# Cross-attention kernel: transposes of the probabilities one by one between a key tile's context products instead of four in a row

## The chip, the cores and the metric

One core of a Trainium2 chip runs the whole program in one launch. The metric is the device time of one execution in microseconds (us), the median over several runs. Engines are called by the profile's names: PE (matrix products and transposes), PEld (the loading of PE's stationary operand, which the profile shows as an engine of its own), DVE, ACT, POOL, and SP, which issues the transfers.

## The reference, cut to what matters

Two layers, each an attention over a context of 1500 rows and a mixture of experts, work on 8 x 56 tokens of 256 channels. The change touches the softmax attention of the first layer only:

```
q = rms_norm((layernorm(x) @ Wq)  per head, 16 heads of 128)
k = rms_norm((ctx @ Wk)           per key head, 4 heads of 128)
v = ctx @ Wv                      4 heads of 128
probs = softmax(q k^T / sqrt(128))            over 1500 context rows
out   = (probs v, heads side by side) @ Wo
x     = x + out
```

All sums are in float32, and every product of full accuracy is made of three passes over operands that are split in a high and a low part.

## The kernel before, in words

The program has three stages: the sums of the second layer's linear attention and all queries; the softmax attention, one batch row after the other (`softmax_attention`); and a tail with the mixtures of experts. The second stage holds the change.

A batch row is worked off in two **units**, u = 0 and u = 1, of eight heads each; there are 16 units. Below, "even" units are those with u = 0 and "odd" ones those with u = 1. Instead of projecting values and then summing, the kernel sums the context rows themselves with the probabilities as weights (the **context products**), and projects the sums afterwards (`output`). A unit runs so:

- `scores` writes 12 tiles of scores (PE) into three banks of PSUM (`ring`). DVE (L1052) moves them to `pr` with the running minimum, ACT (L944) takes the exponentials.
- Then come 12 steps, one for each key tile t of 125 context rows. `turn(t)` transposes the probabilities of tile t with four PE transposes (L877) into bank t % 3 of `ring`. ACT (L960) copies the bank into the high part `pT[0]`, DVE (L1067) subtracts to get the low part `pT[1]`, and with that frees the bank and raises `ring_free`. The context products of step t are two times the three passes of `mm3` (L102 to L104), 448 columns each, into `csum`; PE waits for `ring_free` of tile t before them.
- The transposes run two tiles ahead: step t issues `turn(t + 2)` and then the products of t. `turn(0)` and `turn(1)` stand ahead of the steps, and steps 10 and 11 have none. So 10 groups of four transposes in a unit stand inside a step.
- At the end of most steps stands a piece of the key projection of the next unit, `key_step`, by the list `SEQ`: either six products into `proj` (then ACT L933, DVE L1018 and POOL L1118 square it and split the square), or two products into `mean` (L835), after which ACT takes logarithm and exponential (L938, L940) and DVE (L1021, L1026) and POOL (L1122) make the normalised keys. In odd units DVE also splits the next batch row's context (L998) and queries (L1006, L1009) between these. The last unit has no `key_step`.

Every engine works its list in the written order and is held by semaphores alone. In each step PE's list reads, before the change:

```
if t + 2 < KT:
    turn(t + 2)
wait(pe, ring_free, (2 * b + u) * NR + NSC + t + 1)
...
for i in range(DC):
    last = mm3(nc, csum[:, i, 0:QU], ...)
last.then_inc(pv_done, 1)
if keys and t + 2 < len(SEQ):
    key_step(*keys, *SEQ[t + 2])
```

Of the kernel before, what the change touches and what calls it, by code (L numbers as in the profile page):

```python
# [19 lines left out]
TP = NTOK // TT  # L20
# [3 lines left out]
KT = 12  # L24
KP = SK // KT
# [9 lines left out]
QU = 2 * QG  # L35
# [25 lines left out]
def wait(eng, sem, value):  # L61

    if isinstance(value, int) and value <= 0:
        return
    eng.wait_ge(sem, value)
# [34 lines left out]
def mm3(nc, out, w_hi, w_lo, x_hi, x_lo, start, stop):  # L100

    nc.tensor.matmul(out, w_lo, x_hi, start=start, stop=False, skip_group_check=True)  # L102
    nc.tensor.matmul(out, w_hi, x_lo, start=False, stop=False, skip_group_check=True)  # L103
    return nc.tensor.matmul(out, w_hi, x_hi, start=False, stop=stop, skip_group_check=True)  # L104
# [631 lines left out]
def softmax_attention(nc, qT, rz, ctx_dram, ctxT_dram, wk, wv, raw_t, ct, kk, q, ident):  # L736
# [8 lines left out]
    with ExitStack() as ctx:  # L745
        p = Phase(nc, ctx, "att")
        raw_n = p.sb("raw_n", [KP, 2, KT // 2, D])
        cn = [p.sb(f"cn{i}", [KP, KT, D], F32R) for i in range(2)]
# [3 lines left out]
        pr = p.sb("pr", [TP, 4, SK])  # L752
# [4 lines left out]
        pT = [p.sb(f"pT{i}", [KP, 3, QU], F32R) for i in range(2)]  # L757
# [4 lines left out]
        ring = p.ps("ring", [128, 3, 512])  # L762
        csum = p.ps("csum", [128, 2, 512])
# [8 lines left out]
        ring_full, ring_free = p.sem("ring_full"), p.sem("ring_free")  # L772
# [17 lines left out]
        @block.sync  # L790
        def _(sp):
            def load_t(b):
                wait(sp, t_lo, (b - 1) * PIECES)
                for c in range(KC):
                    y = slice(c * CH, (c + 1) * CH)
                    src = ctxT_dram[bass.ds(b, 1), :, y] if not isinstance(b, int) else ctxT_dram[b:b + 1, :, y]
                    sp.dma_start(raw_t[:, c], src.rearrange("a (k p) n -> p (a k) n", p=128)).then_inc(t_loaded[c], 16)

            def load_n(b):
                for half in range(2):  # L800
                    wait(sp, n_lo, (b - 1) * KT + (half + 1) * (KT // 2))
                    rows = slice(half * (SK // 2), (half + 1) * (SK // 2))
                    src = ctx_dram[bass.ds(b, 1), rows, :] if not isinstance(b, int) else ctx_dram[b:b + 1, rows, :]
                    sp.dma_start(raw_n[:, half], src.rearrange("a (j p) c -> p (a j) c", p=KP))\
                        .then_inc(n_loaded[half], 16)

            load_n(0)
            load_t(1)
            load_n(1)
            with sp.Fori(2, B) as b:  # L810
                load_t(b)
                load_n(b)

        @block.tensor
        def _(pe):
            def key_step(b, u, part, i):


                n = (2 * b + u - 1) * NS + i
                c, g = i // 2, 2 * u + i % 2  # L820
                if part == 0:
                    if u == 0 and i % 2 == 0:
                        wait(pe, t_lo, (b - 1) * PIECES + DC * (c + 1))
                    wait(pe, k_full, n - 1)
                    for d in range(DC):
                        last = mm3(nc, proj[:, i % 2, 0:CH], wk[0][:, d, g * HD:(g + 1) * HD],
                                   wk[1][:, d, g * HD:(g + 1) * HD], ct[0][:, c, d, :], ct[1][:, c, d, :], d == 0, d == DC - 1)
                    last.then_inc(proj_done, 1)
                else:
                    wait(pe, sq_lo, n + 1)  # L830
                    wait(pe, ln_done, n)
                    if i == 0:
                        wait(pe, out_free, 2 * b + u - 1)
                    for half in (1, 0):
                        last = nc.tensor.matmul(mean[:, 0:CH], mean_mat[:], sq[half][:, i % 2, :],  # L835
                                                start=(half == 1), stop=(half == 0))
                    last.then_inc(mean_done, 1)

            def output(b, u, ahead=NS):


                wait(pe, cs_lo, (2 * b + u + 1) * DC)
                wait(pe, ln_done, (2 * b + u) * NS + ahead)
                wait(pe, out_free, 2 * b + u)
                for gi in range(2):
                    w = slice((2 * u + gi) * HD, (2 * u + gi + 1) * HD)
                    x = slice(gi * QG, (gi + 1) * QG)
                    for i in range(DC):
                        last = mm3(nc, mean[:, x], wv[0][:, i, w], wv[1][:, i, w],
                                   cs[0][:, i, x], cs[1][:, i, x], i == 0, i == DC - 1)  # L850
                last.then_inc(out_full, 1)

            def scores(b, u):

                for j in range(4):
                    gi = j // 2
                    for c in range(KC):
                        r = (2 * b + u) * NR + j * KC + c
                        if j % 2 == 0:
                            wait(pe, k_lo, (2 * b + u - 1) * NS + 2 * c + gi + 1)  # L860
                        if u == 0 and j == 0 and c == 0:
                            wait(pe, q_lo, 2 * b)
                        wait(pe, ring_free, r - 2)
                        h = 8 * u + 2 * j
                        mm3(nc, ring[0:TP, c, 0:CH], q[0][:, h:h + 2, :], q[1][:, h:h + 2, :],
                            kk[:, c, gi, :], kk[:, c, 2 + gi, :],
                            True, True).then_inc(ring_full, 1)

            def unit(b, u, keys, before):


                def turn(t):
                    if t % TPC == 0:
                        wait(pe, exp_done, (2 * b + u) * NE + 3 + t // TPC + 1)
                    wait(pe, ring_free, (2 * b + u) * NR + NSC + t - 2)
                    for j in range(4):
                        last = nc.tensor.transpose(ring[0:KP, t % 3, j * TP:(j + 1) * TP],  # L877
                                                   pr[:, j, t * KP:(t + 1) * KP], ident[0:TP, 0:TP])
                    last.then_inc(ring_full, 1)

                if keys:
                    key_step(*keys, *SEQ[0])
                    key_step(*keys, *SEQ[1])
                turn(0)
                turn(1)
                if before:
                    output(*before)
                for t in range(KT):  # L890
                    if t + 2 < KT:
                        turn(t + 2)
                    wait(pe, ring_free, (2 * b + u) * NR + NSC + t + 1)
                    if u == 0:
                        wait(pe, n_lo, b * KT + t + 1)
                    if t == 0:
                        wait(pe, cs_lo, (2 * b + u) * DC)
                    for i in range(DC):
                        last = mm3(nc, csum[:, i, 0:QU], cn[0][:, t, i * 128:(i + 1) * 128],
                                   cn[1][:, t, i * 128:(i + 1) * 128], pT[0][:, t % 3, :], pT[1][:, t % 3, :],  # L900
                                   t == 0, t == KT - 1)
                    last.then_inc(pv_done, 1)
                    if keys and t + 2 < len(SEQ):
                        key_step(*keys, *SEQ[t + 2])

            def batch(b, first, last):
                scores(b, 0)
                unit(b, 0, (b, 1), None if first else (b - 1, 1))
                scores(b, 1)
                unit(b, 1, None if last else (b + 1, 0), (b, 0))  # L910

            pe.wait_ge(eps_set, 4)
            batch(0, True, False)
            with pe.Fori(1, B - 1) as b:
                batch(b, False, False)
            batch(B - 1, False, True)
            output(B - 1, 1, 0)
# [1285 lines left out]
```

## Time and profile before

| what | value |
|---|---|
| median of 3 runs | 1297.81 us (1297.76 to 1299.46) |
| the profiled execution's own time | 1295.38 us |
| its span, first to last instruction | 1293.7 us |
| mean granted TensorE clock | 0.967 |
| PE busy / PEld busy | 1185.8 us (92%) / 1042.6 us (81%) |
| DVE / ACT / POOL busy | 885.6 (68%) / 731.8 (57%) / 537.9 us (42%) |
| transposes L877 | 768, of 112x112 |
| context products L102 to L104 | 1152, of 125x448 |

Matrix instructions are pipelined: a new one starts before the one ahead of it has ended, so the distance from start to start tells what an instruction costs, and the duration doesn't. The softmax attention lies between about 372 and 1042 us of the span.

### The profile page before, as it was taken

The page shows a single profiled execution, that of the slowest core. Times are in us where ns is not written, and L with a number is a line of the kernel's source. Part 1 is how long each engine was busy: PE and PEld are TensorE (multiplying, and loading weights), DVE is VectorE, ACT ScalarE, POOL GpSimd, SP SyncE. Part 2 cuts the span into 40 slices and gives each one's busy share as a digit, 9 for nine tenths or more (in the row PEclk, how much of TensorE's full clock was granted, in tenths as well). Part 3 has the DMA queues.
Part 4 walks back from the last instruction along what each step waited for, and adds up shares of the span by engine and source line. Part 5 has one row for each costly group of instructions (what it writes and reads, how often), then busy time and mean ns, then how long its engine had stood idle before and what let it go on. Part 6 is the DMA issues. An engine that isn't in the chain of part 4 may idle for free. (4 is left out here: it accounts for less than half of the span.)

```text
span 1293.7 us, 27038 instructions
## 1 busy us (share of the span) xinstructions
PE 1185.8 (92%) x9589; PEld 1042.6 (81%) x9589; DVE 885.6 (68%) x1829; ACT 731.8 (57%) x1285; POOL 537.9 (42%) x559
## 2 busy tenths in 40 slices
PE   5999999999978999999999999999999967897698
PEld 4888888889757878888788887888888866795597
DVE  5665566566656888788878778788886657555654
ACT  4655555566545666666566675766656533342453
POOL 2423232223135354463643636436455146363252
PEclk9999999999988999999999999999999978798799
DMA  4211111110022111011010110111000061004000
GB/s 142 73 42 46 50 32 40 55 40 1 2 69 76 49 42 55 1 47 47 24 44 28 47 47 6 41 47 47 0 0 1 1 224 39 7 26 177 1 1 15
DMA packets 38795, 56.04 MB, mean 43 GB/s; under 512 B 3106, under 2 KB 37202, under 8 KB 38226
## 3 DMA queue, kind: packets, MB, share of 16 engines
q1 hardware_dynamic: 37922, 54.23, 13.2%
q10 hardware_dynamic: 816, 1.05, 0.3%
q8 instruction: 36, 0.59, 0.2%
q14 instruction: 21, 0.17, 0.0%
HBM read 54.81 MB, written 0.46 MB: 43 GB/s over the span
## 5 line engine op out<-in xcount | busy, mean ns | idle before, releaser
L1118 POOL TENSOR_TENSOR att_sq<-att_work,att_sq 128x500 fp32r<-128x500 f32 x90 | 119.7, 1330 | 159.9 <-DVE att_sq L1018 159.9
L1122 POOL TENSOR_TENSOR attention_kk<-att_work,attention_kk 128x500 fp32r<-128x500 f32 x90 | 121.9, 1354 | 153.0 <-DVE attention_kk L1026 153.0
L102 PE MATMUL att_csum<-att_pT,att_cn 125*128 125x448 f32 x384 | 155.9, 406 | 5.7 <-DVE att_pT L1067 5.0
L944 ACT ACTIVATE att_pr<-att_pr,att_nmx 112x1500 f32<-112x1500 f32 (+1 forms) x96 | 108.4, 1130 | 72.5 <-DVE att_nmx L1055 72.5
L104 PE MATMUL att_csum<-att_pT,att_cn 125*128 125x448 f32 x384 | 140.9, 367 | 0.0
L103 PE MATMUL att_csum<-att_pT,att_cn 125*128 125x448 f32 x384 | 140.0, 364 | 0.0
L535 DVE SCALAR_TENSOR_TENSOR attention_kk<-kvs_keys_ps,kvs_bk,attention_kk 64x500 fp32r<-64x500 f32 x96 | 70.8, 738 | 92.2 <-ACT attention_kk L419 90.6
L1067 DVE TENSOR_TENSOR att_pT<-att_ring,att_pT 125x448 fp32r<-125x448 f32 x192 | 118.1, 616 | 21.4 <-ACT att_pT L960 21.2
L1052 DVE TENSOR_SCALAR_CACHE_REDUCE att_pr<-att_ring 112x500 f32<-112x500 f32 x192 | 121.7, 675 | 6.1 <-PE att_ring L104 4.6
L290 PE MATMUL kvs_feat<-kvs_f,attention_kk 128*125 128x256 f32 x768 | 113.3, 285 | 11.1 <-DVE kvs_kp L607 10.1
L877 PEld LDWEIGHTS att_ring<-all_ident,att_pr 112*125 112x125 f32 x768 | 110.2, 189 | 14.5 <-ACT att_pr L944 2.2
L419 ACT ACTIVATE attention_kk<-kvs_keys_ps,kvs_bk 64x500 fp32r<-64x500 f32 x96 | 64.8, 674 | 93.0 <-PE kvs_keys_ps L104 91.8
L960 ACT ACTIVATE att_pT<-att_ring 125x448 fp32r<-125x448 f32 x192 | 102.4, 533 | 22.1 <-PE att_ring L877 22.1
L877 PE MATMUL att_ring<-all_ident,att_pr 112*125 112x112 f32 x768 | 110.8, 270 | 1.8 <-ACT att_pr L944 1.8
L290 PEld LDWEIGHTS kvs_feat<-kvs_f,attention_kk 128*125 128x125 f32 x768 | 98.9, 187 | 16.2 <-issue 14.1
L933 ACT ACTIVATE att_work<-att_proj,att_eps 128x500 f32<-128x500 f32 x90 | 60.7, 674 | 86.6 <-PE att_proj L104 86.6
L1021 DVE TENSOR_TENSOR att_work<-att_proj,att_work 128x500 f32<-128x500 f32 x90 | 60.9, 676 | 55.4 <-ACT att_work L940 54.9
L102 PE MATMUL att_ring<-attention_kk,attention_q 128*112 128x500 f32 x192 | 77.9, 405 | 17.9 <-DVE att_pr L1052 12.6
L472 ACT ACTIVATE kvs_kp<-kvs_feat,kvs_zero 125x512 f32<-125x512 f32 x96 | 65.9, 686 | 42.9 <-PE kvs_feat L290 42.3
L938 ACT ACTIVATE att_work<-att_mean,att_eps 128x500 f32<-128x500 f32 x90 | 61.0, 678 | 45.5 <-PE att_mean L835 45.4
L102 PEld LDWEIGHTS att_csum<-att_pT,att_cn 125*128 125x128 f32 x384 | 73.0, 190 | 15.7 <-DVE att_pT L1067 10.2
L1018 DVE CAST att_sq<-att_work 128x500 fp32r<-128x500 f32 x90 | 51.6, 573 | 39.8 <-ACT att_work L933 39.8
(279 smaller groups left out, 3264.0 us busy)
## 6 DMA issues: line engine op xcount, KB each, us to landing
attention_raw_t<-in_ctxT SPq DMA_DIRECT2D x45, 500.0 KB, 4.0
att_raw_n<-in_ctx SPq DMA_DIRECT2D x16, 750.0 KB
tail_gate_w<-in_gate SPq DMA_DIRECT2D x1, 2112.0 KB, 8.0
tail_up_w<-in_up SPq DMA_DIRECT2D x1, 2112.0 KB, 12.8
kvs_raw_q<-in_wq SPq DMA_DIRECT2D x8, 256.0 KB, 4.0
tail_wo_raw<-in_wo SPq DMA_DIRECT2D x4, 512.0 KB, 6.3
tail_down_w<-in_down SPq DMA_DIRECT2D x1, 2048.0 KB, 17.8
tail_gate_w<-in_gate SPq DMA_DIRECT2D x1, 1760.0 KB, 10.7
```

Source lines behind the costliest of these rows:

```text
L102: nc.tensor.matmul(out, w_lo, x_hi, start=start, stop=False, skip_group_check=True)
L103: nc.tensor.matmul(out, w_hi, x_lo, start=False, stop=False, skip_group_check=True)
L104: return nc.tensor.matmul(out, w_hi, x_hi, start=False, stop=stop, skip_group_check=True)
L290: last = nc.tensor.matmul(feat[0:KP, half, z], ks[:, c, 2 * half + g, y], f2[:, w, :], start=(w == 1), stop=(w == 0), skip_group_check=True)
L535: nc.vector.scalar_tensor_tensor(ks[64:128, c, 2 * m + h, :], keys_ps[y, 0:CH], bk[y, m:m + 1], ks[0:64, c, 2 * m + h, :].bitcast(F32), AL ...
L877: last = nc.tensor.transpose(ring[0:KP, t % 3, j * TP:(j + 1) * TP], pr[:, j, t * KP:(t + 1) * KP], ident[0:TP, 0:TP])
L944: nc.scalar.activation(pr[:, j, keys], pr[:, j, keys], ACT.Exp, scale=-1.0, bias=nmx[:, j:j + 1], accum_out=z[:, 4 * u + j, c:c + 1]).then ...
L960: nc.scalar.activation(pT[0][:, t % 3, :], ring[0:KP, t % 3, 0:QU], ACT.Copy).then_inc(pT_hi, 1)
L1052: nc.vector.tensor_scalar(pr[:, j, c * CH:(c + 1) * CH], ring[0:TP, c, 0:CH], -1.0, 3.0e38, ALU.mult, ALU.min, accum_out=mn[:, j, c:c + 1] ...
L1067: nc.vector.tensor_tensor(pT[1][:, t % 3, :], ring[0:KP, t % 3, 0:QU], pT[0][:, t % 3, :].bitcast(F32), ALU.subtract).then_inc(ring_free, 1)
L1118: nc.gpsimd.tensor_tensor(sq[1][:, i % 2, :], work[:, i % 2, :], sq[0][:, i % 2, :].bitcast(F32), ALU.subtract).then_inc(sq_lo, 1)
L1122: nc.gpsimd.tensor_tensor(kk[:, c, 2 + gi, :], work[:, i % 2, :], kk[:, c, gi, :].bitcast(F32), ALU.subtract).then_inc(k_lo, 1)
```

## The change

`turn` is taken apart into its waits (`turn_ready`) and one transpose (`turn_part`). In a step, the waits and the first transpose of tile t + 2 come first; the second, third and fourth stand behind the first, second and third pass of the first half (i = 0) of the products of tile t. The number of instructions of each kind, their operands and the signals are the same; `ring_full` is raised by the fourth transpose, which now stands behind three context products. The wait for `ring_free` of tile t now stands ahead of three of the four transposes. `turn(0)` and `turn(1)` stay as they are.

```diff
-                def turn(t):
+                def turn_ready(t):
                     if t % TPC == 0:
                         wait(pe, exp_done, (2 * b + u) * NE + 3 + t // TPC + 1)
                     wait(pe, ring_free, (2 * b + u) * NR + NSC + t - 2)
+
+                def turn_part(t, j):
+                    return nc.tensor.transpose(ring[0:KP, t % 3, j * TP:(j + 1) * TP],
+                                               pr[:, j, t * KP:(t + 1) * KP], ident[0:TP, 0:TP])
+
+                def turn(t):
+                    turn_ready(t)
                     for j in range(4):
-                        last = nc.tensor.transpose(...)
+                        last = turn_part(t, j)
                     last.then_inc(ring_full, 1)
...
                 for t in range(KT):
-                    if t + 2 < KT:
-                        turn(t + 2)
+                    turning = t + 2 < KT
+                    if turning:
+                        turn_ready(t + 2)
+                        turn_part(t + 2, 0)
                     wait(pe, ring_free, (2 * b + u) * NR + NSC + t + 1)
...
                     for i in range(DC):
-                        last = mm3(nc, csum[:, i, 0:QU], ...)
+                        c_hi, c_lo = (cn[w][:, t, i * 128:(i + 1) * 128] for w in range(2))
+                        to, p_hi, p_lo = csum[:, i, 0:QU], pT[0][:, t % 3, :], pT[1][:, t % 3, :]
+                        nc.tensor.matmul(to, c_lo, p_hi, start=t == 0, stop=False, skip_group_check=True)
+                        if turning and i == 0:
+                            turn_part(t + 2, 1)
+                        nc.tensor.matmul(to, c_hi, p_lo, start=False, stop=False, skip_group_check=True)
+                        if turning and i == 0:
+                            turn_part(t + 2, 2)
+                        last = nc.tensor.matmul(to, c_hi, p_hi, start=False, stop=t == KT - 1,
+                                                skip_group_check=True)
+                        if turning and i == 0:
+                            turn_part(t + 2, 3).then_inc(ring_full, 1)
```

## Rows read from the trace of the kernel before

**Rows 1.** Stretches: us; busy of PE, PEld, DVE, ACT, POOL; granted clock; DMA; GB/s.
```profile
393.20:400.00 6.80, 3.98 (x13) 3.54 (x13) 4.84 (x7) 0.85 (x2) 5.29 (x6) 0.50 0.33 113
400.00:1042.00 642.00, 627.84 (x3328) 543.07 (x3328) 503.36 (x1094) 408.78 (x711) 298.38 (x262) 1.00 0.09 30
```

**Rows 2.** Waits of PEld, 400 to 1018 us: total us, times, longest.
```profile
PEld att_csum L102 <- DVE att_pT L1067: 5.0, 16, 0.5
```

**Rows 3.** Timeline of PE, last unit: start us, duration us, instruction.
```profile
1022.36 0.59 PE L877 MATMUL att_ring<-all_ident,att_pr 112*125 112x112 f32 x4
...
1035.62 0.59 PE L877 MATMUL att_ring<-all_ident,att_pr 112*125 112x112 f32 x4
...
1037.29 0.36 PE L102 MATMUL att_csum<-att_pT,att_cn 125*128 125x448 f32 x1
...
1038.50 0.37 PE L102 MATMUL att_csum<-att_pT,att_cn 125*128 125x448 f32 x1
```

**Rows 4.** Timeline of PEld, last unit: eight transposes' loads, then the output's loads.
```profile
1018.38 0.95 PEld L877 LDWEIGHTS att_ring<-all_ident,att_pr 112*125 112x125 f32 x8 [2.25 <-ACT att_pr L944]
...
1019.36 0.19 PEld L103 LDWEIGHTS att_mean<-att_cs,attention_wv 128*128 128x128 f32 x1
...
1020.48 0.19 PEld L104 LDWEIGHTS att_mean<-att_cs,attention_wv 128*128 128x128 f32 x1
```

**Rows 5.** Timeline, last unit: a last context product and the four loads behind it.
```profile
1027.13 0.37 PE L104 MATMUL att_csum<-att_pT,att_cn 125*128 125x448 f32 x1
1027.13 0.61 PEld L877 LDWEIGHTS att_ring<-all_ident,att_pr 112*125 112x125 f32 x4
```

**Rows 6.** Timeline of an odd unit (batch row 3), its steps 3 and 7.
```profile
695.03 0.62 DVE L1067 TENSOR_TENSOR att_pT<-att_ring,att_pT 125x448 fp32r<-125x448 f32 x1
695.24 0.59 PE L877 MATMUL att_ring<-all_ident,att_pr 112*125 112x112 f32 x4
...
695.70 0.19 PEld L102 LDWEIGHTS att_csum<-att_pT,att_cn 125*128 125x128 f32 x1
...
705.57 0.61 DVE L1067 TENSOR_TENSOR att_pT<-att_ring,att_pT 125x448 fp32r<-125x448 f32 x1
705.64 0.59 PE L877 MATMUL att_ring<-all_ident,att_pr 112*125 112x112 f32 x4
...
706.24 0.19 PEld L102 LDWEIGHTS att_csum<-att_pT,att_cn 125*128 125x128 f32 x1 [0.19 <-DVE att_pT L1067]
```

**Rows 7.** Timeline of the same unit, step 4: [idle time before, and what ended it].
```profile
699.17 0.54 ACT L960 ACTIVATE att_pT<-att_ring 125x448 fp32r<-125x448 f32 x1
...
700.71 0.68 ACT L938 ACTIVATE att_work<-att_mean,att_eps 128x500 f32<-128x500 f32 x1 [1.00 <-PE att_mean L835]
...
702.16 0.68 DVE L1021 TENSOR_TENSOR att_work<-att_proj,att_work 128x500 f32<-128x500 f32 x1 [1.51 <-ACT att_work L940]
```

**Rows 8.** Timeline of the even unit behind it: its step 0, then its step 3.
```profile
729.96 0.62 DVE L1067 TENSOR_TENSOR att_pT<-att_ring,att_pT 125x448 fp32r<-125x448 f32 x1 [0.74 <-ACT att_pT L960]
...
731.22 0.19 PEld L102 LDWEIGHTS att_csum<-att_pT,att_cn 125*128 125x128 f32 x1
...
738.12 0.59 PE L877 MATMUL att_ring<-all_ident,att_pr 112*125 112x112 f32 x4
...
739.41 0.54 ACT L960 ACTIVATE att_pT<-att_ring 125x448 fp32r<-125x448 f32 x1
```

**Rows 9.** Groups of PE's instructions by shape, 372 to 1041 us: busy us, mean ns.
```profile
L103 PE MATMUL att_csum<-att_pT,att_cn 125*128 125x448 f32 x384 | 140.0, 364 | 0.0
L877 PE MATMUL att_ring<-all_ident,att_pr 112*125 112x112 f32 x768 | 110.8, 270 | 1.8 <-ACT att_pr L944 1.8
...
L104 PE MATMUL att_mean<-att_cs,attention_wv 128*128 128x224 f32 x60 | 16.4, 273 | 0.0
```

**Rows 10.** Timeline of the first unit, its steps 0 and 1.
```profile
396.02 0.29 PEld L102 LDWEIGHTS att_csum<-att_pT,att_cn 125*128 125x128 f32 x1 [5.17 <-DVE att_pT L1067]
...
399.26 0.95 PE L877 MATMUL att_ring<-all_ident,att_pr 112*125 112x112 f32 x4
```

More of the change, by code:

```diff
@@ L875, in turn @@
                     wait(pe, ring_free, (2 * b + u) * NR + NSC + t - 2)
+                def turn_part(t, j):
[3 more added lines that the diff above has]
+                    turn_ready(t)
                     for j in range(4):
-                        last = nc.tensor.transpose(ring[0:KP, t % 3, j * TP:(j + 1) * TP],
-                                                   pr[:, j, t * KP:(t + 1) * KP], ident[0:TP, 0:TP])
+                        last = turn_part(t, j)
                     last.then_inc(ring_full, 1)
@@ L898, in unit @@
                     for i in range(DC):
-                        last = mm3(nc, csum[:, i, 0:QU], cn[0][:, t, i * 128:(i + 1) * 128],
-                                   cn[1][:, t, i * 128:(i + 1) * 128], pT[0][:, t % 3, :], pT[1][:, t % 3, :],
-                                   t == 0, t == KT - 1)
+                        c_hi, c_lo = (cn[w][:, t, i * 128:(i + 1) * 128] for w in range(2))
[10 more added lines that the diff above has]
+                            turn_part(t + 2, 3).then_inc(ring_full, 1)
                     last.then_inc(pv_done, 1)
```

## The prediction

> **What bounds the kernel now.** I read the windows by stage first, to see where PE is full and at what clock; then the waits of the load queue, to see what PE stops for; then the timelines of single steps. In the softmax attention from 400 to 1042 us PE is busy 627.84 of 642.00 us at a granted clock of 1.00, the 2.4 GHz level [rows 1]. So this stage is PE's, apart from short waits, and the products of a step stand one behind the other.
>
> What a transpose costs is best read in the last unit, which has no key projection. Eight steps with a group of four start at 1022.36 and 1035.62 us: 13.26 / 8 = 1.658 us a step [rows 3] (the first and the last of nine). Steps without a group are 1038.50 - 1037.29 = 1.21 us apart, which is 0.202 for each of six context products. The group thus costs 0.448 us, 0.112 a transpose.
>
> Why 0.112? The load of a transpose's operand begins with the start of the product ahead of it: both stand at 1027.13 [rows 5]. The four loads there take 0.61 from the first start to the last end; less one load of 0.19 that is 0.42, or 0.20 behind the context product and twice 0.11. So PEld works one load ahead and no further: it idles under a context product although three more loads are due. Among transposes alone the loads start (0.95 - 0.19) / 7 = 0.1086 us apart, and the output's loads of 128 columns (1020.48 - 1019.36) / 10 = 0.112 apart [rows 4]. An instruction's cost is then the longer of the stream ahead of it and its own load.
>
> The second thing to see is where PE waits inside the steps. PEld's first load of the context products waited for DVE's subtraction (L1067) 16 times, 5.0 us in all [rows 2]. In an odd unit the subtraction of tile 3 ends at 695.03 + 0.62 = 695.65 and the load starts at 695.70; that of tile 7 ends at 706.18 and the load starts at 706.24 [rows 6]. Both follow DVE by 0.05, while the transposes of these steps had started at 695.24 and 705.64. So in these two steps PE does its four transposes while it waits for DVE, and is then still early.
>
> **The change, part by part.** It removes nothing and adds no instruction; 160 groups (10 in each of 16 units) are reordered, which moves 480 transposes behind a context product. Its effects are three.
>
> *The pace of PE.* Before, a group costs one load behind a context product (hidden under 0.202) and four exposed ones: three of transposes, one of the first context product. After, each of the four transposes' loads is hidden under a context product, but behind each transpose stands a context product whose load begins only when the transpose starts. Four loads stay exposed, now all of context products. A load that is exposed costs 0.112 instead of 0.1086 if the 128 columns of the output's loads are the nearest row [rows 4]: 3 x 0.0034 x 160 = 1.6 us more. This single alternation is not in the trace, so it is bounded: below by 0; above by giving the whole surplus of a group, 0.448 - 4 x 0.1086 = 0.0136 us, to its one pair of changes between transposes and products, of which the new order has three more: 3 x 0.0136 x 160 = 6.5 us. I take 1.6, since the loads' distances explain it.
>
> The Trainium skill, "TensorE: Matmul & The Clock Gate", section "Architectural detail: the array is 16× 32×32, not 1× 128×128", says that PE's queue of 64 can pull a weight load ahead of products in flight, with which loads could be spread under the longer streams. The trace agrees for one load ahead and shows no second one. With that page's gap for a warm product of N columns (section "Back-to-back issue gap", N / 2.4 + 2.5 ns) a transpose of 112 columns with a hidden load would be estimated at 49 ns, and the sum would be some 640 x 0.06 = 38 us less; by the rows it is nothing less.
>
> *The wait that now stands ahead of three transposes.* PE's wait for tile t is the old one, but queued behind it are now the second to fourth transposes, and behind those ACT's copy and DVE's subtraction of tile t + 2. Where PE was early, the three transposes filled the wait; now they come after it and lengthen the step by 3 x 0.109 = 0.33 us. This holds in steps 3 and 7 of the seven odd units that have a key projection (step 11 waits too, but has no transposes): 14 x 0.33 = 4.6 us. Is it given back? Between the two steps DVE is idle 1.51 us until ACT's exponential, and ACT before that idle 1.00 us until PE's mean product [rows 7]. That product is issued in step 4, behind the lengthened step 3, so ACT, DVE and the subtraction of tile 7 all move by 0.33, and step 7 adds its own; I read the same order from step 8 to the end of the unit and in the scores behind it. Nothing there absorbs it. In even units there is room: the subtraction of tile 0 ends at 730.58 and the products' load starts at 731.22, 0.64 later, more than the 0.33 by which the wait moves forward [rows 8]. Lower bound 0 (all absorbed), upper bound 4.6 for these units.
>
> In the first unit step 0 waits 5.17 us for the same subtraction, at the 1.2 GHz level (0.50) [rows 1, 10]. Three transposes behind it cost 0.33 us at the full clock and about twice that at the low one (four of them last 0.95 there, against 0.59); what slips past 400 us runs at the full clock again. I take 0.4, between 0.33 and 0.66.
>
> *The later signal.* `ring_full` comes three context products later, 3 x 0.202 = 0.61 us. Late next is ACT's copy. In the even unit the transposes end at 738.71 and the copy starts at 739.41, 0.70 later because ACT is at other work [rows 8], so it is not moved. In the odd unit ACT copies tile 6 at 699.17 [rows 7]; 0.61 later it ends at 700.32 at the latest, DVE's 0.61 end at 700.93, and DVE has nothing to do before 702.16. The products that need the tile come two steps later. Cost 0, hidden by DVE's idle time; if that cover were gone, up to 0.61 a step.
>
> Sum: 1.6 + 4.6 + 0.4 = 6.6 us. The profiled execution took 1295.38 us (span 1293.7 and 1.7 around it), so it would take 1302.0; the median of the runs, 1297.81, lies 2.4 above it, and 1297.8 + 6.6 = 1304.4.
>
> **The rivals.**
>
> *Loads hidden after all: faster.* Place: each context product behind a transpose. If its load began before the transpose starts, a transpose would cost only its stream. By duration a transpose (270 ns) equals a product of 224 columns (273), and another 224 columns add 364 - 273 = 91 ns [rows 9], so the stream is about 91 ns against 109: 640 x 0.018 = 11.5 us gained, less the 5.0 of the waits, gives 1291.3. It decides from 8 ns a transpose on. Against it: no load in the trace starts before the product ahead of it. The queue that the page above tells of would be its cause.
>
> *The waits are absorbed: no change.* If DVE, not PE's mean product, set the times of tiles 7 and 11, the 0.33s would only take away waiting. Then 1.6 + 0.4 remain: 1299.8, and 1297.8 if the pace is unchanged too. For it speaks that DVE is the one waited for; against it DVE's idle 1.51 us [rows 7].
>
> *Each change of kind costs.* With the upper bound of the pace, 6.5 instead of 1.6: 1309.3. For it speaks the unexplained part of the 0.0136.
>
> *The late signal reaches the chain.* If one step in each of the 14 units with key projection hands on its 0.61 us, 8.5 more: 1312.9. It decides once DVE's idle time is used up.
>
> **How the numbers follow.** My forecast 0.62, its own range 1302 to 1307; loads hidden 0.05; absorbed 0.13; changes of kind 0.15; late signal 0.05. A measurement of this kernel can tell about 0.2%, 2.6 us, from no change. Slower: 0.62 + 0.15 + 0.05 = 0.82; same 0.13; faster 0.05. The range from 1299.4 to 1310.5 leaves out the faster case, the late signal, and the lower part of the absorbed one, some 0.17.
>
> **What would show it.** Right: loads behind a transpose still 0.11 apart and behind a context product 0.20; the last unit's step at about 1.67 us; in odd units' step 7 PEld idle for about 0.6 us until L1067 (0.19 now [rows 6], and the three loads that stood ahead, some 0.4 with their tail, are gone), in step 3 about 0.5, and its waits for L1067 longer by 0.4 x 14 = 6 us or so; even units as long as before but for the pace. Wrong: a last unit's step below 1.65 us (loads hidden) or above 1.69 (changes cost); the odd units no longer than before (absorbed); ACT's or DVE's waits for `att_ring` or `att_pT` in units other than the last (late signal).

## The result, and the profile after

| what | before | after |
|---|---|---|
| median of 11 runs | 1298.62 us (1297.41 to 1299.91) | 1305.74 us (1300.99 to 1307.3) |
| ratio, 95% interval | | 1.005 (1.004 to 1.006) |
| profiled execution's own time, span | 1295.38, 1293.7 us | 1304.85, 1303.1 us |

The kernel became 0.5% slower, 7.1 us at the medians; 6.6 us were forecast.

Where it went is seen first from the ends of the stage. The list of instructions on the tile `att_csum` gives, for the first pass of the context products, the first and the last start. Before, and then after:

```profile
L102 PEld LDWEIGHTS att_csum<-att_pT,att_cn x384: 186/188/330, 396.0 to 1038.9; 125*128 125x128 f32 x192
```
```profile
L909 PEld LDWEIGHTS att_csum<-att_pT,att_cn x384: 186/190/331, 396.0 to 1045.1; 125*128 125x128 f32 x192
```

Both start at 396.0, and the last one lies 6.2 us later. The profiled executions differ by 9.5 us; the other 3.2 lie behind the attention, where the code is the same and the granted clock was 0.87 before and 0.84 after (windows 1042 to 1293.7 and 1048 to 1303 us). Other kernels below, with the same tail, spread as far, whatever the order of their transposes: from the last copy of the sums to the end of the span it is 1293.7 - 1040.4 = 253.3 us before and 1303.1 - 1046.6 = 256.5 after, but also 1294.5 - 1041.2 = 253.3 in three_in_row, with transposes moved, and 1283.7 - 1026.8 = 256.9 in act_last_tiles, with the old order. So this part goes with the execution and not with the change.

The pace of PE, in the timeline of PEld in the last unit, after (start, duration):

```profile
1028.29 0.18 PEld L878 LDWEIGHTS att_ring<-all_ident,att_pr 112*125 112x125 f32 x1
1028.49 0.19 PEld L909 LDWEIGHTS att_csum<-att_pT,att_cn 125*128 125x128 f32 x1
1028.61 0.19 PEld L878 LDWEIGHTS att_ring<-all_ident,att_pr 112*125 112x125 f32 x1
1028.81 0.19 PEld L912 LDWEIGHTS att_csum<-att_pT,att_cn 125*128 125x128 f32 x1
1028.92 0.19 PEld L878 LDWEIGHTS att_ring<-all_ident,att_pr 112*125 112x125 f32 x1
1029.13 0.19 PEld L915 LDWEIGHTS att_csum<-att_pT,att_cn 125*128 125x128 f32 x1
1029.24 0.19 PEld L878 LDWEIGHTS att_ring<-all_ident,att_pr 112*125 112x125 f32 x1
1029.44 0.19 PEld L909 LDWEIGHTS att_csum<-att_pT,att_cn 125*128 125x128 f32 x1
```

It agrees with [rows 4, 5]: a transpose's load (L878) begins 0.11 to 0.12 after the load of the context product ahead of it, and the next context product's load 0.20 to 0.21 after that. Each of the four transposes hides its load under a context product, and behind each stands a context product whose load is not hidden. The sum is the one of before, but for a little. The first transposes of steps 0 and 8 in PE's timeline, after:

```profile
1026.82 0.27 PE L878 MATMUL att_ring<-all_ident,att_pr 112*125 112x112 f32 x1
...
1040.17 0.26 PE L878 MATMUL att_ring<-all_ident,att_pr 112*125 112x112 f32 x1
```

13.35 / 8 = 1.669 us a step, against 1.658 before [rows 3]: 0.011 us a group.

The wait, in steps 3 and 7 of the odd unit of [rows 6], after:

```profile
697.72 0.61 DVE L1084 TENSOR_TENSOR att_pT<-att_ring,att_pT 125x448 fp32r<-125x448 f32 x1
697.96 0.26 PE L878 MATMUL att_ring<-all_ident,att_pr 112*125 112x112 f32 x1
698.38 0.19 PEld L909 LDWEIGHTS att_csum<-att_pT,att_cn 125*128 125x128 f32 x1 [0.46 <-DVE att_pT L1084]
698.70 0.26 PE L878 MATMUL att_ring<-all_ident,att_pr 112*125 112x112 f32 x1
699.01 0.26 PE L878 MATMUL att_ring<-all_ident,att_pr 112*125 112x112 f32 x1
699.33 0.26 PE L878 MATMUL att_ring<-all_ident,att_pr 112*125 112x112 f32 x1
699.85 0.19 PEld L102 LDWEIGHTS att_proj<-attention_ct,attention_wk 128*128 128x128 f32 x1
...
709.26 0.19 PEld L909 LDWEIGHTS att_csum<-att_pT,att_cn 125*128 125x128 f32 x1 [0.57 <-DVE att_pT L1084]
710.73 0.19 PEld L102 LDWEIGHTS att_proj<-attention_ct,attention_wk 128*128 128x128 f32 x1
```

In step 3 the products still follow DVE's subtraction by 0.05 (697.72 + 0.61, 698.38). One transpose stands ahead of them now; three run behind the wait, where before all four had used it. From the first load of the products to the first load of the key projection it is 699.85 - 698.38 = 1.47 us, and in step 7 710.73 - 709.26 = 1.47. Before, the products' load in step 3 stands at 695.70 [rows 6], and the projection's, in the same timeline, at

```profile
696.83 0.19 PEld L102 LDWEIGHTS att_proj<-attention_ct,attention_wk 128*128 128x128 f32 x1
```

That is 1.13 us: the step is 0.34 longer, the three transposes. That the loss stays is seen from the starts of whole units. `turn(0)` and `turn(1)` are eight transposes in a row in every kernel here, so their rows mark the units. In PE's timeline after, an even unit, the odd one of above, and the one behind it begin at

```profile
647.82 1.02 PE L878 MATMUL att_ring<-all_ident,att_pr 112*125 112x112 f32 x8
688.48 1.02 PE L878 MATMUL att_ring<-all_ident,att_pr 112*125 112x112 f32 x8
732.08 1.02 PE L878 MATMUL att_ring<-all_ident,att_pr 112*125 112x112 f32 x8
```

and before at

```profile
645.27 1.02 PE L877 MATMUL att_ring<-all_ident,att_pr 112*125 112x112 f32 x8
685.79 1.02 PE L877 MATMUL att_ring<-all_ident,att_pr 112*125 112x112 f32 x8
728.67 1.02 PE L877 MATMUL att_ring<-all_ident,att_pr 112*125 112x112 f32 x8
```

The even unit lasts 40.66 instead of 40.52 us, the odd one 43.60 instead of 42.88 (up to the next unit's mark, with the scores between). Seven of each kind make 7 x (0.14 + 0.72) = 6.0 of the 6.2 us.

The waits of PEld for the subtraction, 400 to 1025 us, after (total, times, longest):

```profile
PEld att_csum L909 <- DVE att_pT L1084: 10.4, 23, 0.6
```

5.0 us in 16 waits before [rows 2]. The wait grew by 5.4 us, the attention by 6.2: the waits that the profile counts are a good hint here and no measure.

### The profile page after: what moved, and what is told of

Read it like the earlier page. It is cut to its first block and busy times, and to the rows that moved or that the text cites. A ratio compares the mean times of both kernels' runs of the same rounds, so it can differ in the third digit from the quotient of the medians.

```text
span 1303.1 us, 27038 instructions
## 1 busy us (share of the span) xinstructions
PE 1192.6 (92%) x9589; PEld 1046.2 (80%) x9589; DVE 882.9 (68%) x1829; ACT 736.5 (57%) x1285; POOL 538.1 (41%) x559
## 5 line engine op out<-in xcount | busy, mean ns | idle before, releaser
L878 PE MATMUL att_ring<-all_ident,att_pr 112*125 112x112 f32 x768 | 183.1, 262 | 1.8 <-ACT att_pr L961 1.8
L909 PE MATMUL att_csum<-att_pT,att_cn 125*128 125x448 f32 x384 | 169.9, 442 | 9.8 <-DVE att_pT L1084 9.5
L915 PE MATMUL att_csum<-att_pT,att_cn 125*128 125x448 f32 x384 | 154.5, 402 | 0.0
L912 PE MATMUL att_csum<-att_pT,att_cn 125*128 125x448 f32 x384 | 153.6, 400 | 0.0
L878 PEld LDWEIGHTS att_ring<-all_ident,att_pr 112*125 112x125 f32 x768 | 137.1, 189 | 9.0 <-ACT att_pr L961 2.5
L1035 DVE CAST att_sq<-att_work 128x500 fp32r<-128x500 f32 x90 | 48.4, 537 | 44.3 <-ACT att_work L950 44.3
```

The source lines that it names most:

```text
L878: return nc.tensor.transpose(ring[0:KP, t % 3, j * TP:(j + 1) * TP], pr[:, j, t * KP:(t + 1) * KP], ident[0:TP, 0:TP])
L909: nc.tensor.matmul(to, c_lo, p_hi, start=t == 0, stop=False, skip_group_check=True)
L912: nc.tensor.matmul(to, c_hi, p_lo, start=False, stop=False, skip_group_check=True)
L915: last = nc.tensor.matmul(to, c_hi, p_hi, start=False, stop=t == KT - 1, skip_group_check=True)
```

## The experiments

Seven kernels ran beside the kernel before, each 5 to 12 times. Beside the median stand the lengths of an even and an odd unit, read from the same three marks as above. They are worth more than the totals: they hold neither the tail nor the changes of the granted clock at the two ends of the attention.

| kernel | median us | ratio to before, interval | even unit | odd unit |
|---|---|---|---|---|
| before | 1299.04, 1299.23 | | 40.52 | 42.88 |
| the change | 1305.74 | 1.005 (1.004 to 1.006) | 40.66 | 43.60 |
| wait_only | 1302.97 | 1.0037 (1.0024 to 1.0051) | 40.50 | 43.52 |
| row_at_3_7 | 1301.34 | 1.0018 (1.0009 to 1.0027) | 40.65 | 42.91 |
| changed_dve_order | 1298.74 | 0.9999 (0.9989 to 1.0009) | 40.68 | 42.63 |
| before_dve_order | 1295.36 | 0.9973 (0.9963 to 0.9982) | 40.51 | 42.47 |
| three_in_row | 1298.19 | 0.9995 (0.9983 to 1.0007) | 40.59 | 42.57 |
| second_half | 1299.80 | 1.0005 (0.9992 to 1.0017) | 40.67 | 42.63 |
| act_last_tiles | 1284.18 | 0.9886 (0.9864 to 0.9907) | 40.51 | 40.65 |

(Before has a median for each of the two sets of runs: 1299.04 for wait_only to before_dve_order, 1299.23 for the last three. The ratio of the change is to the 1298.62 of the result.)

**wait_only: the wait alone.** The kernel before, its wait put behind the first transpose; the transposes stay in a row. `turn` takes the numbers of the transposes to issue.

```diff
                     if t + 2 < KT:
-                        turn(t + 2)
+                        turn(t + 2, (0,))
                     wait(pe, ring_free, (2 * b + u) * NR + NSC + t + 1)
+                    if t + 2 < KT:
+                        turn(t + 2, (1, 2, 3))
```

> The kernel before with one change: the wait for tile t stands behind the first transpose of its group instead of behind the fourth; the four transposes stay in a row, ahead of the products. Theory (the wait holds back three transposes in steps 3 and 7 of the odd units): nearly all of the loss is there, 14 x 0.33 = 4.6 us and some 0.1 to 0.4 in the first unit, so 4.5 to 5 us slower than before, about 1303.4; the last unit's step stays 1.658 us. Rival (each alternation of transposes and products costs some 0.04 us a group): no alternation is added, so no change, 1298.6. Rival (the later signal is what costs): the signal is not later in steps without a wait, so no change either.

Measured: 3.9 us slower. Even units are unchanged (40.50), odd ones 0.64 longer, 0.32 a step. In PEld's timeline of step 3 of the same odd unit the loads of the three transposes are seen to start with the end of the wait:

```profile
696.30 0.18 PEld L878 LDWEIGHTS att_ring<-all_ident,att_pr 112*125 112x125 f32 x1
697.00 0.40 PEld L878 LDWEIGHTS att_ring<-all_ident,att_pr 112*125 112x125 f32 x3 [0.51 <-DVE att_pT L1071]
697.33 0.19 PEld L102 LDWEIGHTS att_csum<-att_pT,att_cn 125*128 125x128 f32 x1
```

697.33 - 697.00 = 0.33 us stand between the end of the wait and the products. Not one transpose stands between products here, and the larger part of the loss is there: 7 x 0.64 = 4.5 us. Both rivals expected none.

**row_at_3_7: the change without the two steps.**

```diff
                     turning = t + 2 < KT
+                    if u == 1 and t in (3, 7):
+                        turn(t + 2)
+                        turning = False
                     if turning:
```

> The changed kernel, but in steps 3 and 7 of the units with u = 1 the four transposes stand in a row ahead of the wait, as before; the other groups stay taken apart. Theory (wait): 14 x 0.33 = 4.6 us are won back and only the pace remains, 1.6 to 2 us above the kernel before: about 1300.5. Rival (alternation costs): 144 of 160 groups still alternate, so 0.9 of the loss remains: about 1305. Rival (later signal): the same 1305, as the signal is late in all other steps.

Measured: 2.3 us above before, where 1.6 to 2 were expected and the rivals said 1305 us. Odd units are back to 42.91, though eight of their ten groups are still taken apart; even ones keep their 40.65. So 16 of 160 groups, 14 of them with a wait, hold the greater part of the loss. In the odd units the pace costs nearly nothing either (0.03), which I had not expected: most groups there lie in stretches at whose end PE waits for DVE anyway. Steps 3 and 7 of the same odd unit show it (DVE's subtraction, then the products' first load):

```profile
696.98 0.61 DVE L1087 TENSOR_TENSOR att_pT<-att_ring,att_pT 125x448 fp32r<-125x448 f32 x1
697.65 0.19 PEld L912 LDWEIGHTS att_csum<-att_pT,att_cn 125*128 125x128 f32 x1
...
707.52 0.61 DVE L1087 TENSOR_TENSOR att_pT<-att_ring,att_pT 125x448 fp32r<-125x448 f32 x1
708.18 0.19 PEld L912 LDWEIGHTS att_csum<-att_pT,att_cn 125*128 125x128 f32 x1
```

The loads follow DVE by 0.06 and 0.05 us, and lie 708.18 - 697.65 = 10.53 us apart, against 706.24 - 695.70 = 10.54 before [rows 6], although the groups of steps 4 to 6 are taken apart.

**changed_dve_order and before_dve_order: the wait taken away.** In both, DVE splits the next queries behind the subtraction of tiles 3 and 7 instead of ahead of it.

```diff
                     if t == 0 and before:
                         output(*before)
+                    if u == 1 and keys and t in (3, 7):
+                        split_q(keys[0], (3, 7).index(t))
                     if keys and t >= 1:
                         key_step(*keys, *SEQ[t])
...
-                    if u == 1 and keys and t in (2, 6):
-                        split_q(keys[0], (2, 6).index(t))
```

> The changed kernel, and on DVE the splitting of the next queries (L1006, L1009 of the kernel before) stands behind the subtraction of tiles 3 and 7 instead of ahead of it, so that the subtractions come about 2 us earlier and PE has no wait in these steps. Theory (wait): the loss of 4.6 us goes, and with it the waits of 0.13 and 0.27 us that the kernel before has there, 7 x 0.40 = 2.8; what remains against the kernel before is 1.6 + 0.2 - 2.8, so about 1 us faster than before, 1297.6. Rival (alternation costs): only the 2.8 are won, 1303. If the later split holds up the key chain, it is slower than that by what the same edit costs in the kernel before.

> The kernel before with the same DVE order alone: subtraction of tiles 3 and 7 ahead of the splitting of the queries. Theory: PE's waits in steps 3 and 7 of seven odd units go, 7 x 0.40 = 2.8 us faster than before, about 1295.8, and the changed kernel with this DVE order stands 1.6 to 2 us above this one. Rival (alternation costs): the two stand 6.5 us apart. If DVE's wait only moves to another tile: no change, 1298.6.

Measured: with the changed order of the transposes the time falls from 1305.74 to 1298.74 us, with the old order it falls to 1295.36, 0.27% under before. Now the two orders differ by 3.4 us instead of 7.1; by the units it is 7 x (0.17 + 0.16) = 2.3. Expected were 1297.6 and 1295.8, 1.6 to 2 us apart: the first came out 1.1 higher, and the intervals, about 1.3 us to either side for each of the two, don't tell 3.4 from 2.3. PEld's waits for the subtraction, 400 us to the end of the stage, in changed_dve_order and then in before_dve_order:

```profile
PEld att_csum L909 <- DVE att_pT L1084: 3.4, 9, 0.4
```
```profile
PEld att_csum L102 <- DVE att_pT L1067: 3.7, 9, 0.5
```

The same nine waits in both: those of steps 3 and 7 are gone, and with them what the order of the transposes had done to the odd units. What is left, 0.16 to 0.17 in the units of the table, is ten groups at about 0.016 us.

**three_in_row: one alternation instead of three**, on changed_dve_order.

```diff
                         if turning and i == 0:
                             turn_part(t + 2, 1)
+                            turn_part(t + 2, 2)
+                            turn_part(t + 2, 3).then_inc(ring_full, 1)
                         nc.tensor.matmul(to, c_hi, p_lo, start=False, stop=False, skip_group_check=True)
-                        if turning and i == 0:
-                            turn_part(t + 2, 2)
...
-                        if turning and i == 0:
-                            turn_part(t + 2, 3).then_inc(ring_full, 1)
```

> The changed kernel with the later query split on DVE (changed_dve_order), but the second to fourth transposes stand in a row behind the first pass of the products: one alternation more than in the kernel before, not three. Theory (each further pair of changes between transpose and product costs some 4 ns): the last unit's step lies a third of the way, 1.662 us between 1.658 (four in a row) and 1.669 (one by one); total about 1 us above before_dve_order, 1296.4. Rival (the surplus has to do with the first transpose standing alone, or with the wait): the step stays 1.669, total 1298.7.

The last unit's step, from the first transposes in PE's timeline:

```profile
1026.53 0.26 PE L878 MATMUL att_ring<-all_ident,att_pr 112*125 112x112 f32 x1
...
1036.50 0.26 PE L878 MATMUL att_ring<-all_ident,att_pr 112*125 112x112 f32 x1
```

9.97 / 6 = 1.662 us, as expected, and the units lie between the two neighbours (even 40.51, 40.59, 40.68). So the surplus grows with the number of alternations and has not to do with the first transpose standing alone. The total of 1298.19 is 1.8 us more than expected and can't tell it from changed_dve_order. In the profiled execution a stretch of the last unit had the lower clock, unlike before; windows of three_in_row and then of before (us, busy of PE, PEld, DVE, ACT, POOL, granted clock, DMA, GB/s):

```profile
1015.00:1026.00 11.00, 9.19 (x52) 8.45 (x51) 6.06 (x16) 5.91 (x13) 0.00 (x0) 0.84 0.01 2
```
```profile
1015.00:1026.00 11.00, 9.19 (x61) 8.21 (x60) 7.33 (x20) 6.42 (x15) 0.00 (x0) 1.00 0.01 2
```

With the same 9.19 us of busy PE, 52 of its instructions lie in the stretch instead of 61: part of it ran at the 1.2 GHz level. In both kernels PE had been idle 1.81 us for the last unit's exponential just before. This doesn't explain the 1.8 us: the profiled execution itself took 1296.23 us. Why the median lies higher stays open.

**second_half: the signal later still**, on changed_dve_order: the second to fourth transposes behind the passes of the second half.

```diff
-                        if turning and i == 0:
+                        if turning and i == 1:
```

(in all three places)

> The changed kernel with the later query split on DVE, and the second to fourth transposes behind the passes of the second half (i = 1) of the products: as many alternations, but the signal to ACT comes another 0.61 us later, 1.22 us later than in the kernel before. Theory (lateness has slack on ACT, DVE and in the two steps to the use): the same as changed_dve_order up to 0.2 us a unit, 1298.7 to 1302. Rival (the late signal reaches the chain): 0.61 us in each of 14 units, 8.5 us more, 1307.

Measured: units of the same length as changed_dve_order (40.67 and 42.63). DVE's waits for ACT's copy, 400 to 1018 us, in changed_dve_order and then here:

```profile
DVE att_pT L1084 <- ACT att_pT L977: 18.1, 32, 1.0
```
```profile
DVE att_pT L1084 <- ACT att_pT L977: 45.5, 63, 2.3
```

DVE waits 27 us more and the units are no longer. Even 1.22 us of lateness is hidden by the two steps between a transpose and its use.

**act_last_tiles: what stands behind the odd unit.** With PE's waits in steps 3 and 7 gone, DVE's row of work from the last key product to the scores has no break, as its timeline in before_dve_order shows:

```profile
713.44 0.68 DVE L1021 TENSOR_TENSOR att_work<-att_proj,att_work 128x500 f32<-128x500 f32 x1 [0.25 <-ACT att_work L940]
714.15 0.42 DVE L1026 CAST attention_kk<-att_work 128x500 fp32r<-128x500 f32 x1
714.49 3.05 DVE L998 CAST att_cn<-att_raw_n 125x256 fp32r<-125x256 f32 x4
717.46 0.67 DVE L1052 TENSOR_SCALAR_CACHE_REDUCE att_pr<-att_ring 112x500 f32<-112x500 f32 x1
```

Here ACT makes three of the four copies, on before_dve_order:

```diff
+                if u == 1 and keys:
+                    n = keys[0]
+                    wait(act, n_loaded[1], 16 * (n + 1))
+                    wait(act, n_hi, n * KT + KT - 3)
+                    for t in range(KT - 3, KT):
+                        nc.scalar.activation(cn[0][:, t, :], raw_n[:, 1, t - KT // 2, :], ACT.Copy).then_inc(n_hi, 1)
...
-                if u == 1 and keys:
-                    for t in range(KT - 3, KT):
-                        split_n(keys[0], t)
```

> The kernel before with the DVE order of before_dve_order, and the high parts of the next batch row's last three context tiles, which DVE copies behind the odd unit (four copies of L998 take 3.06 us there, while POOL works), are copied by ACT behind its own copies of the sums. If DVE sets the end there, as the unbroken row of DVE work from the last key product to the scores says, about 2 to 2.8 us a batch row are won in seven batch rows: 14 to 19 us, 1276 to 1281. If the keys' low part from POOL or PE's scores set it: 1290 to 1295. If nothing moves: 1295.4.

Measured: 1284.18 us, 1.1% under before and 11.2 us under before_dve_order. Odd units lose 1.82 us, less than the 2 to 2.8 expected, and the total misses its 1276 to 1281; DVE is now idle 0.82 us for PE's scores instead:

```profile
709.09 0.28 DVE L1004 CAST att_cn<-att_raw_n 125x256 fp32r<-125x256 f32 x1
710.20 0.68 DVE L1058 TENSOR_SCALAR_CACHE_REDUCE att_pr<-att_ring 112x500 f32<-112x500 f32 x1 [0.82 <-PE att_ring L104]
```

This has nothing to do with the order of the transposes, but it is the version that beats both kernels, and it follows from asking at each wait of PE what DVE was doing.

## Why the prediction was right

The direction, the range and the sum hold: 6.6 us forecast; 7.1 measured at the medians (the interval of the ratio is about 5 to 8 us), 6.2 in the attention of the profiled executions. The signs named beforehand came: PEld idle 0.46 us in step 3 and 0.57 in step 7 (0.5 and 0.6 forecast), 5.4 us more of its waits (6), a last unit's step of 1.669 us (1.67). Step by step:

- *The wait ahead of three transposes*, forecast 4.6 us, is confirmed by leaving everything else away (wait_only, 4.5 us by the units), by leaving it alone away (row_at_3_7, odd units back within 0.03) and by taking its cause away (the DVE order). That it isn't given back was argued from DVE's idle 1.51 us [rows 7]; the unbroken shift of the units' marks shows it.
- *The pace*, forecast 1.6 us between 0 and 6.5, came out within its bounds and near the value taken: 0.014 to 0.016 us a group where PE sets the pace, 0.011 in the last unit. That the total is near is in part luck, for two errors offset each other. I took 3 x 0.0034 = 0.010 us a group, which is about a third too little; and I had it in all 160 groups, but in the change the odd units pay little of it (0.03 us a unit in row_at_3_7, at most 0.72 - 0.64 = 0.08 by wait_only). About nine units of ten groups make 1.3 us. In changed_dve_order, where PE sets the pace in the odd units too, all pay.
- *The first unit*, forecast 0.4 us: the mark of the second unit lies at 435.95 us after and at 435.74 before, 0.2 later, which includes ten groups at 0.014. But this mark spreads over 1.9 us among the nine kernels (435.24 in wait_only, which has the same wait, to 437.14 in row_at_3_7), with the low clock at the unit's start. So whether the wait costs 0.4 here or nothing isn't shown.
- *The later signal*, forecast 0, is confirmed by second_half. But the sign that I named for it was a bad one. ACT's waits for the transposes did grow, from 10.4 us in 14 to 30.6 in 46 waits (400 to 1018 us), and DVE's for ACT's copy from 11.1 to 18.0, outside the last unit, and nothing was lost: waits of an engine with time to spare say nothing.
- *Loads hidden after all* is out: no load begins ahead of the product before it, after as before. *Changes of kind cost* is out at its upper bound, 0.041 us a group. As a small effect it can't be told from the term that I took, a context product's load exposed in place of a transpose's: both go with the number of alternations (three_in_row), and which of the two the 0.014 is stays open. *The waits are absorbed* is out by wait_only; the 1297.8 given there with an unchanged pace leaves out the first unit's 0.4 and should be 1298.2, which changes nothing.

Of the difference at the medians 0.9 us isn't seen in the attention. It lies within the interval, and the tail's spread between executions, 253.3 to 256.9 us, is larger; it was not followed further.

## What to carry to other kernels

If the load of a stationary operand runs one instruction ahead and no further, alternating short and long products doesn't hide loads: the short one's load is hidden, the long one's behind it is not, and the sum stays. Before a wait is moved forward in an engine's list, look at whether the instructions that it passes were filling it; work that stands ahead of a wait is free as long as the wait lasts. And a wait that the profile shows on the bound engine is better asked about on the engine that it waits for: two lines moved there gave 0.27%, and three copies moved off it 0.9% more.

## What the runs showed of the hardware that was not expected

- The granted clock at the two ends of the attention differs between executions of nearly the same program: from 393 to 400 us it was between 0.51 and 0.76. Behind an idle time of PE of 1.81 us, which all nine profiled executions have, the last unit had the lower level, 1.2 GHz, for a while in three of them (granted clock 0.84 in three_in_row and second_half from 1015 to 1026 us, 0.89 in act_last_tiles from 1000 to 1015). In three_in_row it then lasts from its first transposes at 1017.61 us to the last context products at 1039.8, 22.2 us, against 1038.9 - 1018.38 = 20.5 before. Differences of 1 to 2 us between kernels are therefore read from units in the middle, where the clock was 1.00 in all nine (410 to 1000 us).
- A context product behind a single transpose takes 0.11 to 0.12 us from its load to the next one, about as much as behind the fourth of a row (695.70 to 695.81 before). The single alternation, which the trace of before could not show, costs some 4 to 5 ns (0.011 to 0.016 us a group for three more).
